# Attention scores from two fp16 pieces, two heads in the two row halves of the array, in an fp32 transformer layer

## The reference

```
h = layernorm(x)
q = rope((h @ Wq) as 32 heads of 16);  k = rope((h @ Wk) as 8 heads of 16);  v = (h @ Wv) as 8 heads of 16
scores = q . k / sqrt(16)          # four q heads share one k and v head; causal
x = x + layernorm((softmax(scores) @ v) @ Wo)
x = x + layernorm(shared_expert(layernorm(x)) + routed_experts(layernorm(x)))   # 64 experts, top 6
```

## Time and profile before

| | us |
|---|---|
| three timed runs, median | 2481.25 (2466.48 to 2498.78) |
| profiled execution, first to last instruction | 2509.0 |
| PE busy | 2128.5 (85%) |
| DVE busy | 1436.8 (57%) |
| ACT busy | 1096.3 (44%) |
| POOL busy | 714.2 (28%) |
| DVE reductions of maxima, L995 | 738.0 |
| PE maxima matmuls L468 and mask L472 | 462.7 and 207.9 |
| PE transposed scores L571 | 377.4 |
| PE outputs L557 | 323.2 |

### The profile page before, as it was taken

How to read it: one execution, slowest core, us unless ns; L and a number is a source line. 1 busy time by engine, 2 the same in 40 slices (tenths; PEclk the granted TensorE clock), 3 DMA queues, 4 the chain that set the end, 5 groups by cost and what they waited for, 6 DMA issues and landing times.

```text
span 2509.0 us, 42445 instructions
## 1 busy us (share of the span) xinstructions
PE 2128.5 (85%) x12192; PEld 1066.8 (43%) x12192; DVE 1436.8 (57%) x3106; ACT 1096.3 (44%) x1600; POOL 714.2 (28%) x819
## 2 busy tenths in 40 slices
PE   6799988987999898979998989799979687888840
PEld 4433335554333255643333546333336344444420
DVE  7677745676777355767773648777726311111138
ACT  3466663344666533546664335466643221212210
POOL 3111113631111145311111453111115422222238
PEclk9799999997999999979999999799999898999975
DMA  3022222310000022000000210000002299999988
GB/s 126 1 85 84 84 101 99 141 45 5 10 9 9 29 84 82 20 5 9 9 9 30 66 60 14 5 9 9 9 30 69 89 284 265 286 301 292 283 251 293
DMA packets 138751, 231.58 MB, mean 92 GB/s; under 512 B 24423, under 2 KB 57191, under 8 KB 138640
## 3 DMA queue, kind: packets, MB, share of 16 engines
q1 hardware_dynamic: 111792, 191.07, 23.6%
q0 software_dynamic: 24576, 35.07, 5.8%
q10 hardware_dynamic: 2272, 4.06, 0.4%
HBM read 141.59 MB, written 126.48 MB: 107 GB/s over the span
## 4 chain that ended last, share of the span: by engine, by line
PE 63%; issue 12%; DVE 9%; DMA 8%; DVEq 3%; ACT 3%; POOL 2%; POOLq 1%; SPq 0%; ACTq 0%
PE ps L557 10%; PE ps L571 9%; PE ps L468 9%; DMA gx<-dispatch_scratch 6%; PE ps L694 5%; PE ps L444 5%; PE ps L641 4%; DVE rmax L995 3%; PE ps L667 3%; PE ps L726 3%; PE ps L459 2%; PE ps L680 2%; DVEq L1001 2%; PE ps L472 2%; PE ps L445 2%
## 5 line engine op out<-in xcount | busy, mean ns | idle before, releaser
L995 DVE TENSOR_REDUCE rmax<-ps 128x1 f32<-128x512 f32 (+3 forms) x1216 | 738.0, 658 | 282.3 <-PE ps L472 216.5
L827 ACT ACTIVATE pr<-ps 128x1024 f32<-128x1024 f32 (+3 forms) x768 | 593.0, 808 | 329.1 <-PE ps L571 328.2
L468 PE MATMUL ps<-kT,qT 96*128 (+3 forms) x1536 | 462.7, 345 | 52.4 <-DVE rmax L995 49.0
L571 PE MATMUL ps<-qT,kT 98*128 (+3 forms) x1536 | 377.4, 333 | 22.8 <-DVEq L287 10.5
L1279 POOL TENSOR_SCALAR_AFFINE_SELECT pr<-pr 128x512 f32<-128x512 f32 x256 | 162.4, 635 | 778.2 <-ACT pr L827 778.2
L557 PE MATMUL ps<-pr,v_ones 128*32 128x512 f32 (+3 forms) x3072 | 323.2, 500 | 1.4 <-POOL pr L1279 1.2
L468 PEld LDWEIGHTS ps<-kT,qT 96*128 (+1 forms) x1536 | 151.9, 99 | 274.2 <-issue 133.2
L571 PEld LDWEIGHTS ps<-qT,kT 98*128 (+1 forms) x1536 | 112.6, 98 | 286.4 <-issue 184.7
L1322 POOL DMA_INDIRECT dispatch_scratch<-x,slot_i x192 | 189.4, 987 | 70.4 <-issue 56.9
L472 PE MATMUL ps<-causal,id_b 128*128 128x128 bf16 x1024 | 207.9, 228 | 0.0
L694 PE MATMUL ps<-gu_sb,gxT 128*128 128x384 f32 x512 | 203.4, 524 | 0.0
(11 more groups left out here) (138 smaller groups left out, 2519.8 us busy)
## 6 DMA issues: line engine op xcount, KB each, us to landing
gu_sb<-w_gu_dram SPq DMA_DIRECT2D x64, 768.0 KB, 6.8
dn_sb<-w_dn_dram SPq DMA_DIRECT2D x64, 384.0 KB, 10.4
dispatch_scratch<-blank SPq DMA_DIRECT2D x8, 2308.0 KB, 7.9
gx<-dispatch_scratch SPq DMA_DIRECT2D x64, 288.5 KB, 6.2
xin<-x_dram SPq DMA_DIRECT2D x32, 256.0 KB, 2.7
acc_scratch<-blank SPq DMA_DIRECT2D x32, 256.0 KB, 2.1
xres<-x_dram SPq DMA_DIRECT2D x32, 256.0 KB, 3.1
x_scratch<-x SPq DMA_DIRECT2D x32, 256.0 KB, 2.0
```

Source lines behind the costliest of these rows:

```text
L468: last = pe.matmul(o, qT[0:QROWS, half, bass.ds(REP * g + h, 1), q % QPH * P:(q % QPH + 1) * P].squeeze(1), kT[0:QROWS, bass.ds(g, 1), kh ...
L571: last = pe.matmul(ps[:, 2 + 2 * pair + h, 0:HALF - c0], kT[0:BROWS, bass.ds(g, 1), kt * P:(kt + 1) * P].squeeze(1), qT[0:BROWS, qh, bass. ...
L827: act.activation(pr[i % SLOTS][:, 2 * pair:2 * pair + 2, 0:HALF - c0], ps[:, 2 + 2 * pair:4 + 2 * pair, 0:HALF - c0], ACT.Exp, scale=HD ** ...
L995: dve.tensor_reduce(dst[:, heads[0]:heads[0] + n, q % QPH], ps[:, bank, 0:n * w].rearrange("p (h k) -> p h k", k=w), AX, ALU.max).then_inc ...
```

## The change

Both operands get two fp16 pieces (high and low) instead of three bf16, and three products of pieces (high x high, low x high, high x low) instead of six: 48 rows (`SROWS`), 50 with the two rows of the maximum. Two q heads share a column block of `qT`: the even one in rows 0 to 63, the odd one in rows 64 to 127; k stands in both halves. So `qT` and the transposes before it have half as many blocks (three times eight per tile, 128 columns each). The matmuls of two heads are written one behind the other, for the two halves of the rows. Units come in pairs (`PAIRS`), 40 units per group, each pair in two banks; the banks are still 0, 1 and 7. The mask on a diagonal takes two matmuls of 64 rows (128 and 64 columns). `highs` on ScalarE and `lows` on POOL fill the stacks. `rows` issues four DMAs instead of two, since the halves are apart. Weights are scaled by powers of two at the start so that fp16 holds the values, and the exponential's factor undoes it from a register. TensorE's loop over groups is unrolled; the other engines keep theirs. `ysh` moves to another place in SBUF.

```diff
-PIECES = 6
-QROWS = PIECES * HD
-BROWS = QROWS + 2
+SROWS = 3 * HD
+BROWS = SROWS + 2
+ROWT = 64
...
-                n = {128: 4, 256: 2, 384: 1, 512: 1}[w]
-                for h in range(0, REP, n):
-                    out.append((half, q, kh, w, tuple(range(h, h + n))))
+                if 2 * w <= HALF:
+                    out += [(half, q, kh, w, (parity, parity + 2)) for parity in range(2)]
+                else:
+                    out += [(half, q, kh, w, (h,)) for h in range(REP)]
...
                     for part in range(2):
-                        sp.dma_start(qT[QROWS + part:QROWS + part + 1, half, bass.ds(REP * g, REP), :],
-                                     mT[half][16 * part:16 * part + 16, :]).then_inc(max_rows[half], 16)
+                        for parity in range(2):
+                            row = ROWT * parity + SROWS + part
+                            sp.dma_start(qT[row:row + 1, half, bass.ds(2 * g, 2), :],
+                                         mT[half][16 * part + 8 * parity:16 * part + 8 * parity + 8, :]).then_inc(max_rows[half], 16)
...
+                def score_unit(g, units):
 
-                    half, q, kh, w, heads = UNITS[u]
-                    for k, h in enumerate(heads):
-                        o = ps[:, bank, k * w:(k + 1) * w]
-                        diag = q // QPH == kh
-                        last = pe.matmul(o, qT[0:QROWS, half, bass.ds(REP * g + h, 1), q % QPH * P:(q % QPH + 1) * P].squeeze(1),
-                                         kT[0:QROWS, bass.ds(g, 1), kh * HALF:kh * HALF + w].squeeze(1),
-                                         start=True, stop=not diag)
-                        if diag:
-                            last = pe.matmul(o[:, w - P:w], id_b[:], causal[:], start=False, stop=True)
-                    last.then_inc(sc_done, 1)
+                    done = []
+                    for k in range(len(UNITS[units[0][0]][4])):
+                        stage = []
+                        for u, bank in units:
+                            half, q, kh, w, heads = UNITS[u]
+                            h = heads[k]
+                            r = ROWT * (h % 2)
+                            o = ps[:, bank, k * w:(k + 1) * w]
+                            diag = q // QPH == kh
+                            last = pe.matmul(o, qT[r:r + SROWS, half, 2 * g + h // 2, q % QPH * P:(q % QPH + 1) * P],
+                                             kT[r:r + SROWS, g, kh * HALF:kh * HALF + w], start=True, stop=not diag)
+                            if diag:
+                                stage.append((o, r, w))
+                            elif k == len(heads) - 1:
+                                last.then_inc(sc_done, 1)
+                        for o, r, w in stage:
+                            pe.matmul(o[:, w - P:w], sel[r:r + ROWT, 0, :], above[r:r + ROWT, r:r + P],
+                                      start=False, stop=False)
+                        for o, r, w in stage:
+                            last = pe.matmul(o[:, w - ROWT:w], sel[r:r + ROWT, 1, :], above[r:r + ROWT, r:r + ROWT],
+                                             start=False, stop=True)
+                            if k == len(heads) - 1:
+                                last.then_inc(sc_done, 1)
...
                             for h in range(2):
+                                r = ROWT * h
                                 last = pe.matmul(ps[:, 2 + 2 * pair + h, 0:HALF - c0],
-                                                 kT[0:BROWS, bass.ds(g, 1), kt * P:(kt + 1) * P].squeeze(1),
-                                                 qT[0:BROWS, qh, bass.ds(REP * g + 2 * pair + h, 1), c0:HALF].squeeze(1),
+                                                 kT[r:r + BROWS, g, kt * P:(kt + 1) * P],
+                                                 qT[r:r + BROWS, qh, 2 * g + pair, c0:HALF],
                                                  start=True, stop=True)
...
-                with pe.Fori(0, KVH - 1) as g:
-                    group(g, True)
-                group(KVH - 1, False)
+                for g in range(KVH):
+                    group(g, g < KVH - 1)
...
+            qk_w = ((0, wqkv_sb[:, :, 0:H * HD]), (1, wqkv_sb[:, :, H * HD:NQK]))
+            dve.wait_ge(weights_in, 16 * 3)
+            for j, w in qk_w:
+                last = dve.tensor_reduce(wmax[:, j:j + 1], w, mybir.AxisListType.XY, ALU.max, apply_absolute_value=True)
...
+            for j, w in qk_w:
+                dve.tensor_scalar(w, w, wscale[:, j:j + 1], None, ALU.mult)
+            dve.drain().then_inc(scale_ready, 1)
...
-                    dve.tensor_tensor(rot[k][:], rot_a[:], rot_b[:], ALU.add)
-                    dve.drain()
-                    dve.tensor_copy(stk[k][:, :, 0:HD], rot[k][:]).then_inc(high_ready, 1)
-                    dve.drain()
-                    first = stk[k][:, 0:H, 0:HD]
-                    dve.tensor_copy(stk[k][:, 0:H, HD:2 * HD], first)
-                    dve.tensor_copy(stk[k][:, 0:H, 2 * HD:3 * HD], first)
...
+                    dve.tensor_tensor(rot[k][:], rot_a[:], rot_b[:], ALU.add).then_inc(rot_ready, 1)
...
```

246 lines of the change are left out of this document (143 added, 103 removed).

## The result

The changed kernel takes 2632.6 us (median of four runs, 2613.89 to 2655.53), the kernel before on the same chip 2490.02: 1.057 times as long, 95% interval 1.049 to 1.064. Medians in this document are of all runs, while ratios leave out the runs that lie over 1.5% above the fastest of their kernel, so a ratio is not the quotient of two medians. The profiled execution spans 2634.3 us against 2509.0 before, 125.3 us more.

What follows compares the result with a forecast made beforehand. Attention was taken as bound by TensorE (30.32 of 31.54 us per group). Attention -9, projection -26 and start +5 gave -30 us on the 2481 median: 2451 us, -1.2%, range 2375 to 2545.

Steps and rivals of the forecast that it cites:

- 28 x -0.3 = -9 us: Attention: 28 groups, each 31.2 us against 31.54, together save 9 us.
- chance 0.14, 2549 us: Attention rival: clock falls where TensorE waits for VectorE, +3.5 us per group, +68 in all, 2549 us; chance 0.14.
- Step: 1.20 + 1.54 = 2.74 us: Wide attention step: 1.20 us from first to second maxima pair, 1.54 to the next first; 2.74 against 3.01.
- Sum 31.2 us: One attention group, gaps between the starts of its 20 maxima pairs added up: 31.2 us against 31.54.
- 0.9 us for the rows: Attention, before the first wide step: TensorE waits 0.9 us per group for the transposed maxima to land.
- Two heads at once: Score matmuls in attention: a 512-column pair in row halves takes 0.22 us, saving 7.9 us of TensorE time per group.
- the halves do not run together: Score-matmul rival: pairs take 0.44 us, a group 34.6, the kernel 2547 us; chance 0.08.
- The banks hold less: Attention rival: gaps between maxima pairs near 1.2 us, a group 28.5 instead of 31.2, kernel 2376 us; chance 0.30.
- Projection: Projection stage: fewer copies and transposes save 6.4 us per batch, 26 us over four batches.
- The switch: Projection: changing the array's shape around lone maxima units, priced at 0.25 us; +3.5 us with the mask.
- Start: Kernel start: memset of kT goes, weights must be reduced and scaled; first TensorE work at 20.3, +5 us once.
- The maxima's rows: Attention: four DMAs per half-sequence instead of two, 0.6 us per issue, landing 1.7 us later.

Runs made afterwards that it cites:

- run 3: Changed kernel with the two matmuls of a pair in the same row half, so one after the other; 1.136 times the kernel before.
- run 6: Kernel before with TensorE's group loop unrolled, maxima over 48 of 96 rows, transposed scores over 34 of 98; 1.212 times the kernel before.
- run 9: Changed kernel with 64 rows instead of 48 and 50 in every score matmul, output unchanged; 1.016 times the kernel before.
- run 8: Changed kernel with 23 extra transposed-score pairs per group where TensorE waits, and two row DMAs per half-sequence instead of four; 0.987 times the kernel before.
- run 1: Changed kernel with transposed-score matmuls of the second pair of heads in every step issued three times; 1.014 times the kernel before.
- run 12: Changed kernel with 64 rows, 11 extra transposed-score pairs per group, and two row DMAs per half-sequence instead of four; 0.985 times the kernel before.
- run 2: Changed kernel with transposed-score matmuls of both pairs of heads issued twice; 1.027 times the kernel before.
- Run 10: Kernel before with groups unrolled and maxima over 48 of 96 rows, transposed scores left at 98; 1.180 times the kernel before.

## Why the prediction was wrong, and where it was right

**The step that failed** is the sum's silent condition that attention stays at a clock share of 0.98; it had 0.66 (649.3 to 935.2). The term that carries it is "28 x -0.3 = -9 us": measured, 28 x +6.0 = +168. It stood among the rivals (chance 0.14, 2549 us), and there with the wrong mechanism: "Afterwards TensorE waits for VectorE in steps 4 to 6 of every group, too", and against it, "in the middle of the group before, TensorE waited at 1.00 without losing the clock". I had read the 0.58 of the last stretch of projection as caused by the waits there, and asked of every gap only how long TensorE is idle. Waits are not needed: run 3 and run 6 have the low clock with TensorE busy 97% and more, run 9 a higher one with more idle time. They still count: filling them keeps the clock (run 8). The change halves the rows of the score matmuls, so per group the array gets about half the score work that it had. What the prediction left out is that this alone can cost the clock.

**The size of that rival** was off too. The price of a wide step at the lower level was about right (4.5 worked out, 4.22 measured). But I let two such steps in a group stay low (+3.5 us), and it was over two thirds of the group (+6.0). 28 x 6.0 = 168 us instead of 98.

The Trainium skill (TensorE: Matmul & The Clock Gate, Part 1) says that the gate opens by how busy TensorE has been of late. The prediction reasoned with the profile's busy time, too ("TensorE is nearly always at work"). By that reading run 3's group would run at 2.4 GHz; it had 0.54. The rows of this case decide: the busy column of the profile does not forecast the clock for matmuls on part of the rows.

**The forecast without the clock** held for the step: "Step: 1.20 + 1.54 = 2.74 us", 2.71 in both run 1 and run 12. "Sum 31.2 us" for a group is less well borne out than run 8's 31.14 makes it look: that has its waits filled, which cost 0.7 us, and two DMAs for each set of rows, not four. Run 12's 30.42 is the nearest measured. It too has two DMAs, and the prediction without its 0.9 us for the rows gives 30.3. No run has the changed kernel's work alone at a clock of 1.00. That the best versions are 1.5% faster than before and the forecast was -1.2% is in part luck, since they are other kernels.

**Two heads at once**: 0.22 us for a pair, as taken (0.39 with latency, as for one alone). The rival "the halves do not run together" is out. By the estimate worked out from the Trainium skill's 3.07 for four row tiles (TensorE: Matmul & The Clock Gate, Part 3) a pair would have taken 0.06 us more; no row here shows it, and two pairs of run 12 follow each other in 0.22 us (204.12, 204.34).

**The banks hold less** (2376 us, chance 0.30): not seen. With the clock at 1.00 and own banks the group is 30.8, with less filling 30.4, not 28.5. Run 12's wide step is held as the prediction had it: its second pair waits 0.35 us for a reduction (205.07). Little filling and own banks together were not run.

**Projection**: -26 us predicted for four batches, -22 measured (-4.0 to -7.0 a batch). Only the sum was tested, not its parts; the clock in the second batch's stage was 0.85 (0.86 before).

**The switch** was priced at 0.25 us from the outputs. In the masks, where it can be read by itself, it is 0.09. A unit alone between full-array matmuls has one change in and one out, 0.18 us by these rows.

**Start**: +5 predicted, +3.8 measured. **The maxima's rows**: four issues take 3.04 to 3.44 us, not 2.4; 0.9 us on the path was not seen, since at the lower clock TensorE came to the first wide step only at 246.00, straight from its outputs. With the clock higher and the four DMAs still there the wait appears: in run 1 TensorE waits for these rows 9 times, 13.5 us in all, and in run 2 8 times, 12.2 us; in run 8 and run 12, with two DMAs, never.

**Not settled**: by which measure of rows and columns the clock moves. Run 10 had both levels with the same work. Why the trace behind the last batch's attention takes 12 us less was not tried either.

## What to carry to other kernels

Halving the rows of small matmuls and packing them side by side works and can still lose: it takes work out of the array, and the clock that the whole engine gets can fall with it. The packing was not at fault: with less of it the same rows did worse (run 3, 1.136). Before such a change, ask what the clock share is and whether the remaining work keeps the array's rows in use; after it, look at an instruction that the change did not touch (here the outputs, 1.93 us for 1.07) before looking at waits. If the clock has gone, widen the slices with rows that are zero anyway (free, 4% here) and fill the waits sparingly (a group of 30.4 us with 11 extra pairs, 31.1 with 23).

## What the runs showed of the hardware

- The granted clock can be low with TensorE never idle: a share of 0.54 with 48.48 of 48.54 us busy (48 and 34 rows), 0.55 with 57.45 of 57.46 (48 and 98 rows). In the same kernel another group with the same instructions has 1.00.
- Rows that hold zeros count for the clock: 64 rows instead of 48 and 50 raised the group's share from 0.64 to 0.85, at no cost in a matmul (0.39 us with latency for 512 columns either way). Rows are not all: with 48 and 50 rows and 23 extra pairs in the waits the share was 1.00.
- Two matmuls in the upper and lower 64 rows take the time of one: 0.39 us with latency for 512 columns, alone or in pairs, and pairs follow each other every 0.22 us.
- A change between a tile of half the array's height and one of the full height costs 0.09 us (0.16 us from one matmul of 128 columns to the next in place of 0.07); between 96 and 128 rows it costs nothing that shows.
- One row and its copy 64 partitions further can be written by one DMA. Two such DMAs take 1.24 us to issue in run 12 (202.19), where four single ones take 3.04 to 3.44 us in the changed kernel.
